# A four-layer graph network on one Trainium2 core: eight gathers of each layer's first step moved in front of the layer boundary

## What is computed

```python
e = edge_attr @ We + be
m = relu(x[src] + e)
agg = segment_sum(m, dst)
h = ((1 + eps) * x + agg) @ W1 + b1
h = (h - mean(h, 0)) * rsqrt(var(h, 0) + 1e-5) * gamma + beta
x = relu(relu(h) @ W2 + b2)
```

## Time and profile before

| | |
|---|---|
| median of 3 runs | 1625.68 us (1625.5 to 1625.84) |
| the profiled execution's own time | 1627.86 us |
| its span, first to last instruction | 1626.1 us |
| PE busy | 1457.9 us (90%) |
| DVE busy | 1305.7 us (80%) |
| POOL busy | 1068.9 us (66%) |
| ACT busy | 280.5 us (17%) |
| mean granted TensorE clock | 0.978 |
| traffic | 327.04 MB, mean 201 GB/s |

### The profile page before, as it was taken

The page is one execution under the profiler, slowest core; times in us unless marked ns, Lnnn a source line. Parts: engine busy times, 40 slices in busy tenths (PEclk is TensorE's granted clock), DMA queues, the critical chain, the costliest instruction groups (busy, mean ns, idle before and its releaser), DMA issues.

```text
span 1626.1 us, 21389 instructions
## 1 busy us (share of the span) xinstructions
PE 1457.9 (90%) x8387; PEld 898.9 (55%) x8387; DVE 1305.7 (80%) x2119; ACT 280.5 (17%) x650; POOL 1068.9 (66%) x1135
## 2 busy tenths in 40 slices
PE   4798899999789989999979898989996989899998
PEld 3355566665455656566435565656543656565563
DVE  7998889876687888787568887888766878888876
ACT  3011111116100010011610110111170100111023
POOL 6777777770477777777067777777507777777740
PEclk9999999999899999999989999999998999999999
DMA  9777777772677777777167777777627777777753
GB/s 326 210 211 210 211 210 211 210 234 77 197 210 211 210 212 210 211 211 236 52 220 211 211 210 210 212 210 211 202 70 233 211 210 211 210 211 210 210 172 129
DMA packets 108271, 327.04 MB, mean 201 GB/s; under 512 B 20763, under 2 KB 21915, under 8 KB 108165
## 3 DMA queue, kind: packets, MB, share of 16 engines
q0 software_dynamic: 90080, 295.25, 62.7%
q1 hardware_dynamic: 18084, 30.36, 5.5%
HBM read 312.73 MB, written 12.80 MB: 200 GB/s over the span
## 4 chain that ended last, share of the span: by engine, by line
POOL 31%; issue 10%; PE 9%; DVE 1%; DMA 1%; ACT 0%; DVEq 0%; POOLq 0%
POOL rows L464 31%; PE y_ps L1335 6%; PE pair_ps L1185 1%; DMA rows<-node_table,src_all 1%; PE h_ps L1279 1%; PE y_ps L1346 1%; DVE rows L876 0%; PE y_ps L1230 0%; PE y_ps L1290 0%; DMA node_table<-rows 0%; PE uT_ps L1266 0%; PE uT_ps L1242 0%; PE uT_ps L1259 0%; DVE mv L902 0%; PE uT_ps L1252 0%
## 5 line engine op out<-in xcount | busy, mean ns | idle before, releaser
L464 POOL DMA_INDIRECT rows<-node_table,src_all x1110 | 1049.6, 946 | 494.9 <-issue 336.9
L876 DVE SCALAR_TENSOR_TENSOR rows<-We_ps,negw_all,rows 128x512 f32<-128x512 f32 x1126 | 768.8, 743 | 222.1 <-DMA rows<-node_table,src_all 219.7
L1230 PE MATMUL y_ps<-table_parts,src_onehot 128*128 128x512 f32 x2520 | 686.3, 416 | 20.5 <-DVE src_onehot L782 20.5
L1230 PEld LDWEIGHTS y_ps<-table_parts,src_onehot 128*128 128x128 f32 x2520 | 464.7, 194 | 280.4 <-issue 166.1
L1185 PE MATMUL pair_ps<-rows,onehot 128*32 128x512 f32 x2504 | 344.7, 616 | 130.0 <-DVE rows L876 129.5
L1185 PEld LDWEIGHTS pair_ps<-rows,onehot 128*32 128x32 f32 x2504 | 51.9, 109 | 246.0 <-issue 135.9
L782 DVE TENSOR_TENSOR src_onehot<-y_ps,src_bc 128x1280 fp32r<-128x1280 f32 x126 | 186.5, 1482 | 0.0
L573 ACT COPY pair_sb<-pair_ps 128x512 f32<-128x512 f32 x80 | 46.9, 586 | 632.1 <-PE pair_ps L1185 632.1
L1279 PEld LDWEIGHTS h_ps<-uT,W_sb 128*128 128x128 f32 x1184 | 135.2, 192 | 32.2 <-issue 32.2
L1279 PE MATMUL h_ps<-uT,W_sb 128*128 128x128 f32 x1184 | 142.7, 278 | 0.5 <-DVE w_sum L831 0.5
L1335 PE MATMUL y_ps<-rows,hT 128*128 128x512 f32 x288 | 124.6, 593 | 1.5 <-ACT hT L653 1.5
(11 more groups left out here) (114 smaller groups left out, 651.4 us busy)
## 6 DMA issues: line engine op xcount, KB each, us to landing
rows<-node_table,src_all POOLq DMA_INDIRECT x1110, 3.7
node_table<-rows SPq DMA_DIRECT2D x29, 256.0 KB
x_now<-x_pad SPq DMA_DIRECT2D x10, 512.0 KB, 7.4
W_sb<-W SPq DMA_DIRECT2D x4, 1024.0 KB, 6.1
rows<-W SPq DMA_DIRECT2D x16, 256.0 KB
out<-rows SPq DMA_DIRECT2D x8, 256.0 KB
node_table<-rows SPq DMA_DIRECT2D x8, 224.0 KB
be_bc<-be SPq DMA_DIRECT2D x5, 256.0 KB, 8.5
```

What stands on the lines that cost most here:

```text
L464: nc.gpsimd.indirect_dma_start(rows[:, slot, :], None, source, bass.IndirectOffsetOnAxis(places[:, t:t + 1], 0)).then_inc(landed[q], 16)
L876: last = nc.vector.scalar_tensor_tensor(rows[:, slot, :], We_of, negw_all[:, t:t + 1], row, ALU.mult, ALU.max)
L1230: last = nc.tensor.matmul(y_ps[k % 2][:, :], src_onehot[:, k % 2, b, :], table_parts[:, part, b, :], start=(part, b) == PRODUCTS[0], stop= ...
```

## The change

Line numbers here are those of the kernel before unless a row of the changed kernel's order shows its own.

- **Early gathers.** In layers 1 to 3, eight tiles of step 0 (slots 13 and 12; 11, 10 and 3; 0, 1 and 2) are gathered during the dense part of the layer before, once six, seven and eight blocks of `ORDER` are in `node_table` (`EARLY`, `gather_early`). A source whose block isn't written yet is replaced by a row of zeros behind the table (`ZERO_ROW`, `early_src`). PE computes those missing rows from one-hots and `table_parts` (`make_early_rows`: 6, 4, 4, 4, 6, 6, 8 and 8 products, 46 in all), and DVE adds them to what was gathered (`add_early`) before it makes the messages. Seven of the small one-hots are made by DVE in the dense part, between the blocks, the eighth behind quad 0.
- **One tile less on PE.** Step 0 of layers 1 to 3 keeps two such tiles, of quads 4 and 7; that of quad 1 goes to POOL. Their one-hots and products come later in step 0.
- **The start.** Quad 7 of the very first step is gathered from `x_pad` too.
- **Parameters.** `eps_cur`, `vec` and `W1_sb` of the next layer are loaded during the dense part, once the scales are ready (for layer 0: at the start, W1 when the table is written); `b2_bc` and `be_bc` in the third step of the layer.
- **Scales.** The features go in three groups (128, 128, 256) instead of two, the last `h` block uses other banks, and the W2 products no longer wait for its copies out of the banks.

```diff
+        if i == 0:
+            return (4, 7)
...
+    ORDER = [BLOCKS - 1] + list(range(BLOCKS - 1))
+    ZERO_ROW = N
+    EARLY = [(6, [13, 12]), (7, [11, 10, 3]), (8, [0, 1, 2])]
+    WRITTEN = [written for written, _ in EARLY] + [BLOCKS]
+    SLOT_TILE = {slot: (tile, q) for q, quad in enumerate(FULL) for slot, tile, _ in quad}
+    EARLY_TILES = {SLOT_TILE[slot][0] for _, slots in EARLY for slot in slots}
+    EARLY_COLUMNS, GROUP_COLUMNS = {}, []
+    for _, slots in EARLY:
+        first = len(COLUMNS) + len(EARLY_COLUMNS)
+        for slot in sorted(slots):
+            EARLY_COLUMNS[slot] = len(COLUMNS) + len(EARLY_COLUMNS)
+        GROUP_COLUMNS.append((first, first + len(slots)))
+    ALL_COLUMNS = len(COLUMNS) + len(EARLY_COLUMNS)
+    MISSING = {slot: ORDER[written:] for written, slots in EARLY for slot in slots}
+    ADD_ORDER = [3, 0, 1, 2, 10, 11, 12, 13]
+    ONEHOT_AT = {3: (1, 0), 0: (1, 3), 1: (1, 5), 2: (1, 7), 10: (0, 0), 11: (0, 3), 12: (0, 6), 13: (1, 0)}
+    AGAIN = 7
+    EARLY_QUADS = {0: ADD_ORDER[:4], 2: ADD_ORDER[4:6], 3: ADD_ORDER[6:]}
...
-        shares, done = {}, -2 if l else -1
+        shares, done = {}, 0 if l else -1
...
-    FROM_X = 4
-    LANDINGS = [[[16 * sum(tile not in ON_PE[l][i] for _, tile, _ in quad) for quad in STEPS[i]]
+    FROM_X = (0, 1, 2, 3, QUADS - 1)
...
-            return h_ps[:, 0, :] if c == 0 else y_ps[c - 1][:, 0:P]
+            return [h_ps[:, 0, :], pair_ps[0][:, 0:P], pair_ps[1][:, 0:P], uT_ps[:, 0, :]][c]
...
-        FEW = 2
-        GROUPS = [slice(0, FEW), slice(FEW, C)]
+        GROUPS = [slice(0, 1), slice(1, 2), slice(2, C)]
...
+            load_vectors(0)
...
-                sp.dma_start(eps_cur[:, :], eps[l:l + 1, :].to_broadcast([P, 1])).then_inc(params_loaded, 16)
-                sp.dma_start(vec[:, :, :], vectors[l:l + 1, :, :, :].rearrange("o p v c -> p (o v) c")).then_inc(params_loaded, 16)
-                sp.dma_start(W1_sb[:, :, :], W1[l:l + 1, :, :].rearrange("o (c p) d -> p (o c) d", p=P)).then_inc(params_loaded, 16)
-                sp.dma_start(b2_bc[:, :], b2[l:l + 1, :].to_broadcast([P, D])).then_inc(params_loaded, 16)
-                sp.dma_start(be_bc[:, :], be[l + 1:l + 2, :].to_broadcast([P, D])).then_inc(params_loaded, 16)
+                if l == 0:
+                    for g in range(len(WRITTEN)):
+                        sp.wait_ge(table_written[g], written_count(g, 1))
+                    load_W1(0)
+                sp.wait_ge(quad_summed[7], BLOCKS * l + 3)
+                sp.dma_start(b2_bc[:, :], b2[l:l + 1, :].to_broadcast([P, D])).then_inc(added_loaded, 16)
+                sp.dma_start(be_bc[:, :], be[l + 1:l + 2, :].to_broadcast([P, D])).then_inc(added_loaded, 16)
...
+                    load_vectors(l + 1)
+                    load_W1(l + 1)
...
+            def gather_early(l):
+                pool.wait_ge(zero_written, 16)
+                pool.wait_ge(early_src_ready, 1)
+                for q in EARLY_QUADS:
+                    pool.wait_ge(quad_summed[q], BLOCKS * l + 1)
+                for g, (written, slots) in enumerate(EARLY):
+                    pool.wait_ge(table_written[g], written_count(g, l + 1))
+                    pool.wait_ge(x_updated, BLOCKS * (l - 1) + written + 1)
+                    for slot in slots:
+                        k = EARLY_COLUMNS[slot] - len(COLUMNS)
+                        nc.gpsimd.indirect_dma_start(
+                            rows[:, slot, :], None, table[:, :],
+                            bass.IndirectOffsetOnAxis(early_src[:, k:k + 1], 0)).then_inc(early_landed[slot], 16)
...
+                    if l:
+                        gather_early(l)
...
+            def early_bank(e):
+                return [uT_ps[:, :, :].rearrange("p c n -> p (c n)"), h_ps[:, :, :].rearrange("p c n -> p (c n)"),
+                        y_ps[0][:, :], y_ps[1][:, :]][e % 4]
+            def make_early_onehot(e):
+                slot = ADD_ORDER[e]
+                (buffer, at), blocks, k = ONEHOT_AT[slot], len(MISSING[slot]), EARLY_COLUMNS[slot]
+                nc.vector.tensor_tensor(
+                    src_onehot[:, buffer, at:at + blocks, :],
+                    node[:, MISSING[slot][0]:MISSING[slot][-1] + 1].unsqueeze(2).to_broadcast([P, blocks, P]),
+                    src_bc[:, k:k + 1, :].to_broadcast([P, blocks, P]), ALU.is_equal).then_inc(early_onehot_ready, 1)
+            def add_early(l, e):
+                slot = ADD_ORDER[e]
+                dve.wait_ge(early_landed[slot], 16 * l)
+                dve.wait_ge(early_gathered, len(ADD_ORDER) * (l - 1) + e + 1)
+                nc.vector.tensor_tensor(rows[:, slot, :], early_bank(e), rows[:, slot, :],
+                                        ALU.add).then_inc(early_added, 1)
...
+                        if l and i == 0:
+                            if q == 0:
+                                for e in range(4):
+                                    add_early(l, e)
+                            if q in EARLY_QUADS:
+                                summed = sum(len(slots) for p, slots in EARLY_QUADS.items() if p <= q)
+                                dve.wait_ge(early_added, len(ADD_ORDER) * (l - 1) + summed)
                         messages(q, l, i)
+                        if l and i == 0 and q == 0:
+                            make_early_onehot(AGAIN)
+                            add_early(l, 4)
+                            add_early(l, 5)
+                        if l and i == 0 and q == 1:
+                            add_early(l, 6)
+                            add_early(l, 7)
+                            make_src_onehot(l, 0)
+                            make_src_onehot(l, 1)
+                        if l == 0 and i == 4 and q == 1:
+                            make_early_src()
...
-                    if c == FEW:
-                        bn_scales(l, 0)
                     nc.vector.bn_stats(stats[:, c, BLOCKS + 1, :],
                                        hT[:, c, GUARD - MARGIN + (BLOCKS - 1) * P:GUARD + N]).then_inc(stats_done, 1)
+                    for g, f in enumerate(GROUPS[:-1]):
+                        if c == f.stop:
+                            bn_scales(l, g)
...
+                        if 0 < k <= AGAIN:
+                            make_early_onehot(k - 1)
...
+                    if l and i == 0 and q == 0:
+                        make_early_rows(l, 6)
+                        make_early_rows(l, 7)
...
+            def make_early_rows(l, e):
+                slot = ADD_ORDER[e]
+                buffer, at = ONEHOT_AT[slot]
+                pe.wait_ge(early_onehot_ready, len(ADD_ORDER) * (l - 1) + e + 1)
+                if e == 2:
+                    pe.wait_ge(half_added, l)
+                if e == 3:
+                    pe.wait_ge(y_added, BLOCKS * l)
+                if e >= 4:
+                    pe.wait_ge(early_added, len(ADD_ORDER) * (l - 1) + e - 3)
+                products = [(m, b, part) for m, b in enumerate(MISSING[slot]) for part in range(PARTS)]
+                for m, b, part in products:
+                    if e == 0 and part == 0:
+                        pe.wait_ge(lo_ready, BLOCKS * l + ORDER.index(b) + 1)
+                    last = nc.tensor.matmul(early_bank(e), src_onehot[:, buffer, at + m, :], table_parts[:, part, b, :],
+                                            start=(m, part) == (0, 0), stop=(m, b, part) == products[-1])
+                last.then_inc(early_gathered, 1)
...
-                gather_share(l, -1)
+                    gather_share(l, -1)
+                else:
+                    for e in range(6):
+                        make_early_rows(l, e)
...
-                idle_products(uT_ps[:, :, :].rearrange("p c n -> p (c n)"), WARM)
+                idle_products(y_ps[0][:, :], WARM)
                 pe.wait_ge(W2_loaded, 16 * C * (l + 1))
                 for k, (m, c) in enumerate(HR_ORDER[:-C]):
-                    if m < 3 and c == 0:
-                        if m + 1 < C - 1:
-                            pe.wait_ge(h_part_copied, (C - 1) * l + m + 2)
-                        else:
-                            pe.wait_ge(h_copied, BLOCKS * (l + 1) + 1)
```

163 lines of the change are left out of this document (106 added, 57 removed).

## The result

The changed kernel takes **1604.59 us** (median of four runs, 1603.62 to 1605.16) against 1625.76 us for the kernel before beside it (four runs, 1625.5 to 1627.02). The ratio is 0.9868, 95% interval 0.9853 to 0.9882: some 21 us faster. The forecast was 1596.5 us with a range of 1591 to 1606, so the sign and the range hold, and the gain is smaller than forecast by 8.1 us.

A forecast was written before the change was run, and what follows sets the result against it. POOL's gathers at 1.249 us each, plus boundaries, were taken as the bound. 1627.86 - 30.0 - 1.8 + 2.1 + 0.5 = 1598.7 us; with the median 2.2 lower, 1596.5 us, range 1591 to 1606.

The forecast's parts named there:

- Part 1: POOL's table gathers: 24 fewer at 1.249 us each, with the eight early ones hidden before the boundary; -30.0 us.
- Part 5: Last table write at three boundaries, issued with three early gathers still landing: +0.7 us each, +2.1 us in all.
- The prediction's own test: Sign at the boundary: a last table write landing over 3 us after its issue makes the forecast wrong, for rival A.
- rival A: Early gathers aren't free: writes wait behind them (1609.7 us), or DVE instructions make POOL late (1601.9); 1601 to 1610, chance 0.17.
- Part 2: Added PE products and DVE additions after the boundary don't stop POOL: 25 us of slack cover 10.6; 0 us.
- Part 3: Parameter loads moved away from the boundary: 0 us on the chain.
- Part 4: Scales in three groups let W2 begin 0.45 us sooner in four layers: -1.8 us.
- The start: Three more x_pad gathers at the start share transfers with the first table writes: +0.5 us, ends -1.5 and +3.0.

The follow-up runs named there:

- kernel 1: Changed kernel with each early gather moving 64 of 512 columns, the rest read from other table rows; number, order and waits kept: 1599.3 us, ratio 0.9829.
- kernel 6: Changed kernel with the 46 products for missing rows computed twice, the second time over the first: 1605.56 us, ratio 0.9872.
- kernel 8: Changed kernel with the moved parameter loads (eps, vec, W1, and also b2 and be) back at the begin of a layer: 1606.8 us, ratio 0.9882.
- kernel 4: The kernel before with only the scales in three groups added: 1622.44 us, ratio 0.9979.
- kernel 5: Changed kernel with early tiles one block sooner and 66 instead of 46 products for missing rows: 1601.39 us, ratio 0.9858; on another chip 1935.4 us, 0.9905.
- kernel 2: Changed kernel with five early tiles instead of eight, the last group (slots 0, 1, 2) dropped: 1612.4 us, ratio 0.9911.
- kernel 3: Changed kernel with POOL's waits trimmed and reordered so only the last group's semaphore stands behind the last write: 1605.46 us, ratio 0.9874.

## Why the prediction was right, and where its size was off

- **Part 1, gathers off the chain, -30.0 us: right**, 29.9 measured. 1086 gathers at 1.25 us. Its sub-step "the last three therefore end near 818.8, before the boundary's 820.43" was mis-sized. It placed them 1.3 us after the end of W2; they end 2.4 to 2.7 after it. I had given the eighth block's write 2.57 us; it was issued at 804.00 and took 4.1 us to land, and POOL sat idle 1.73 us for it. The group isn't late on the path as such (kernel 1), but it brings its data beside the final write.
- **Part 5, table writes with gathers under way, +2.1 us: the term that was mis-sized.** The mechanism was named rightly. "With three gathers of 256 KB I am nearer to the lower end: +0.7 us, three times." Measured +3.4, +2.5, +1.6, so +7.5 in all, halfway in the bounds of 0 to +5.1 each. (The third is low because the write of the earlier trace rows, with which it is compared, had its last part land 0.89 us late, with a packet of the instruction queue beside it.) Kernel 1 shows where: about 2.1 us per boundary are the traffic, and about 0.6 us POOL's longer way from a landed write to its first gather. This second piece I had no term for. The prediction's own test, a last write landing over 3 us after its issue, speaks for rival A: it took 3.5 to 4.4.
- **Part 2, PE and DVE, 0 us: right**, shown by kernel 6 with twice the products.
- **Part 3, the loads, 0 us: not contradicted**; in kernel 8, with all of them back, the median is 2.2 us higher and the intervals overlap.
- **Part 4, the scales, -1.8 us: right**, 4 x 0.55 = 2.2 us by kernel 4.
- **The start, +0.5 us:** measured +1.2 in this execution. This lies within the scatter of kernels with the same start, 32.4 to 36.0.
- **Rival A was half true.** Its first mechanism, "writes wait behind the gathers as at the start", is what took the 5 us, at less than half of its price of 13.2. Its second does occur, and without a loss: eight of the 24 early gathers took 1.09 to 1.43 us, and kernel 1, whose early gathers are as long, had its write back at 1.70 us. The prediction thought it weaker than a lock, for the median of 948 ns, and was wrong there. Each of the eight ended 0.82 us after the end of a DVE instruction with both inputs in SBUF that was running when the gather began; a gather that meets none takes 0.95. Two of them are the gathers of 799.97 (1.38 us) and 804.17 (1.21 us) shown above, beside these:

```profile
799.84 0.69 DVE L1234 SCALAR_TENSOR_TENSOR rows<-rows,be_bc 128x512 f32<-128x512 f32 x1
...
803.88 0.68 DVE L425 TENSOR_TENSOR table_parts<-rows,table_parts 128x512 fp32r<-128x512 f32 x1
```

The Trainium skill ("SBUF — State Buffer", Who interferes with whom) says that a VectorE instruction with two SBUF inputs contends with a GpSimd instruction that reads SBUF, and that the second one to come waits for the whole of the first. The trace agrees: a gather waits for what is left of the DVE instruction that it meets, which made these eight longer by 0.15 to 0.49 us, and two gathers of kernel 5, where one-hots follow each other without a gap, by 1.1.

## What to carry to other kernels

Work moved off the bound engine into a gap still brings its transfers into that gap. Before pricing it, look which transfer ends the gap, and let the moved transfers end before that one is issued, not only before the gap's end; one step sooner took 2 us off each boundary here, though the time of the whole fell by less than can be told from scatter. Slack that a trace shows in many short waits can be used: 26 added products, and in kernel 6 another 46, some 20 us together, stopped POOL nowhere where 25 us of waits had been read. But it is slack on one chip; where PE was the bound, the kernel with 20 more products per boundary lost its lead.

## What was not expected of the hardware

- A table write of 128 KB landed in 3.5, 4.4 and 3.6 us with three gathers of 256 KB under way, in 1.70 us beside gathers of an eighth of that, and in 1.68 alone. The write begins late more than it moves slowly. In the changed kernel the hardware queue (q1) moved 39 packets from 810.35 to 812.25 us and 136 from 812.25 to 813.55, so most of the write's own began 1.9 us or more after its issue; in the kernel before 143 stood between 819.25 and 819.80, 0.8 us after the issue, and none in front. The two stretches of the changed kernel:

```profile
q1 hardware_dynamic: 39, 0.03, 5.3%
...
q1 hardware_dynamic: 136, 0.12, 27.2%
```

The Trainium skill ("DMA: Bandwidth & Descriptors", SWDGE vs HWDGE vs iDMA) has the DMA engines serve software and hardware queues in turn; the trace agrees in so far as the write is slowed to about twice its time, and doesn't wait for all of the gathers' data.
- A 128 KB write that else takes 1.7 us took 2.57 us (the kernel before, third boundary) and 3.14 us (kernel 2, first boundary) with no gather under way. Both times fifteen of its sixteen parts landed on time and one was late, and both times one 16 KB packet of the instruction queue (1.25 and 1.53 us long) stood on a DMA engine. That it was the same engine isn't shown.
- In the kernels with early gathers 0.70 us of issue passed from POOL's wake to its first full gather at every boundary, and 0.76 to 0.91 from the landed write; in kernel 4 and before 0.26 from the landed write. Trimming the waits took 0.13 off (kernel 3), less data nothing (kernel 1). The traces show what goes with it: the 0.70 stands where a separate wait instruction of POOL's ends the wait, and the 0.26 where the gather itself waits. Both occur in the changed kernel. The write of 804.00 us landed at 808.10 and the early gather that waited for it began at 808.36, without a wait instruction between. Whether a wait carried by the gather would save the 0.6 us per boundary wasn't tested.
- The first table gather stood between 32.4 and 36.0 us in kernels whose start is the same, against 32.84 and 32.98 in before and kernel 4. This scatter of up to 3.6 us, from one execution of each, is as large as most differences looked for here, and hides the worth of the moved loads.
- One of the chips ran the four kernels tried on it 20% longer, with PE at the lower clock level in stretches and pausing without a releaser in the profile. The ratio of the changed kernel to the one before was 0.9868 again, with another bound; that the digits agree is chance (intervals 0.9853 to 0.9882 and 0.9842 to 0.9894).
